# Edge attributes padded to 128 weight rows, and row numbers copied amid the gathers of the group before

## The reference, cut to what matters

```python
def transformer_conv(h, edge_index, edge_attr, Wq, bq, Wk, bk, Wv, bv, We, ...):
    q, k, v = (h @ W.T + b  for each of the three)     # per node, 4 heads of 32
    e = (edge_attr @ We.T)                              # 4 numbers an edge -> 128
    k_j = k[src] + e
    v_j = v[src] + e
    alpha = einsum('ehc,ehc->eh', q[dst], k_j) / sqrt(32)
    ...                                                 # softmax over the edges of a dst
    out = segment_sum(a * v_j, dst)
```

## Time and profile before

| | |
|---|---|
| time, median of 3 runs | 3711.26 us (3694.59 to 3713.19) |
| the profiled execution | 3716.44 us, of which 3714.7 us are its span |
| busy, share of the span | PE 68%, PEld 51%, DVE 61%, ACT 46%, POOL 62% |
| first-layer edge phase | POOL's first gather 332.8 us, PE's last sum 1447.6 us |
| second-layer edge phase | POOL's first copy 2571.3 us, its last 3092.7 us |
| last node phase | POOL's first copy 3133.4 us, its last 3683.8 us |

### The profile page before, as it was taken

How to read it: one execution, slowest core, us unless ns; L and a number is a source line. 1 busy time by engine, 2 the same in 40 slices (tenths; PEclk the granted TensorE clock), 3 DMA queues, 4 the chain that set the end, 5 groups by cost and what they waited for, 6 DMA issues and landing times. The chain is left out here.

```text
span 3714.7 us, 56727 instructions
## 1 busy us (share of the span) xinstructions
PE 2534.6 (68%) x13730; PEld 1902.9 (51%) x13730; DVE 2276.3 (61%) x9172; ACT 1717.7 (46%) x4075; POOL 2310.2 (62%) x2429
## 2 busy tenths in 40 slices
PE   0004999999999996599999999996333442444444
PEld 0003777777777774366666666664333332444444
DVE  8885555666566656487787878783111111777777
ACT  8993222222222222488787888884111111333332
POOL 5554777777777770555555555543777775777775
PEclk9999999999999997799999999997555555565555
DMA  6452233333333331333333334332666664456666
GB/s 204 172 178 78 79 87 88 93 88 87 86 94 87 88 86 43 74 108 103 107 103 105 106 98 107 103 97 79 121 119 123 123 119 98 127 137 143 137 134 120
DMA packets 253887, 401.92 MB, mean 108 GB/s; under 512 B 56515, under 2 KB 165456, under 8 KB 253728
## 3 DMA queue, kind: packets, MB, share of 16 engines
q1 hardware_dynamic: 183670, 265.77, 25.0%
q0 software_dynamic: 63424, 133.57, 17.9%
q10 hardware_dynamic: 6682, 1.46, 0.2%
HBM read 241.74 MB, written 160.29 MB: 108 GB/s over the span
## 5 line engine op out<-in xcount | busy, mean ns | idle before, releaser
L1629 POOL DMA_INDIRECT aggc<-rows,at_nc x392 | 400.9, 1023 | 149.0 <-issue 109.0
L625 POOL DMA_INDIRECT zs<-z_table,at_s x392 | 381.0, 972 | 161.3 <-issue 89.6
L1147 POOL DMA_INDIRECT agg<-rows,at_n x392 | 389.1, 993 | 144.3 <-issue 111.1
L1463 POOL DMA_INDIRECT h2s<-h_table,at_s x392 | 374.5, 955 | 147.7 <-issue 92.6
L625 POOL DMA_INDIRECT zd<-z_table,at_d x392 | 378.2, 965 | 124.8 <-issue 122.3
L1508 PE MATMUL p_sum<-h2s,same 128*128 128x129 f32 x784 | 213.8, 444 | 338.4 <-DMA h2s<-h_table,at_s 283.3
L1212 PE MATMUL p_f<-z_t,w_t 128*128 128x512 f32 x784 | 377.4, 612 | 64.2 <-ACT act L1282 64.0
L1223 PE MATMUL p_f<-w_t,act 128*128 128x128 f32 x3136 | 383.8, 278 | 0.0
L1223 PEld LDWEIGHTS p_f<-w_t,act 128*128 128x128 f32 x3136 | 361.2, 192 | 22.2 <-issue 22.2
L1508 PEld LDWEIGHTS p_sum<-h2s,same 128*128 128x128 f32 x784 | 176.4, 323 | 375.7 <-issue 300.1
L754 ACT ACTIVATE v_sb<-p_v 128x264 f32<-128x264 f32 x196 | 76.7, 392 | 594.1 <-DVE msgs L836 379.7
(11 more groups left out here) (316 smaller groups left out, 6669.3 us busy)
## 6 DMA issues: line engine op xcount, KB each, us to landing
rows<-rows_sb SPq DMA_DIRECT2D x49, 576.0 KB, 3.6
h_table<-h2b SPq DMA_DIRECT2D x49, 516.0 KB, 2.9
rows<-rows_sb SPq DMA_DIRECT2D x49, 516.0 KB
xa<-in_x_dram SPq DMA_DIRECT2D x49, 512.0 KB, 3.8
z_table<-za SPq DMA_DIRECT2D x49, 512.0 KB, 2.9
dst_sb<-dst SPq DMA_DIRECT2D x98, 256.0 KB
xb<-in_x_dram SPq DMA_DIRECT2D x49, 512.0 KB, 4.1
x_table<-x1b SPq DMA_DIRECT2D x49, 512.0 KB, 4.8
```

Of the source, the lines that this page charges most:

```text
L625: pool.indirect_dma_start(out=to[:, slot, k], out_offset=None, in_=z_table, in_offset=bass.IndirectOffsetOnAxis(ap=at[:, slot, k:k + 1], a ...
L1147: pool.indirect_dma_start(out=agg[:, ring, k], out_offset=None, in_=rows0, in_offset=bass.IndirectOffsetOnAxis(ap=at_n[:, ring, k:k + 1], ...
L1463: pool.indirect_dma_start(out=h2s[:, slot, k], out_offset=None, in_=h2_table, in_offset=bass.IndirectOffsetOnAxis(ap=at_s[:, slot, k:k + 1 ...
L1629: pool.indirect_dma_start(out=agg[:, slot, k], out_offset=None, in_=rows1, in_offset=bass.IndirectOffsetOnAxis(ap=at_n[:, slot, k:k + 1], ...
```

## The change

`wea`, `metag` and `ea_tr` get 16 partitions or columns a tile in place of 6 (`EW = P // G = 16`), so that `ea_tr` fills 128 partitions; the ten further columns of each tile in `metag`, and the further rows in `wea`, hold zeros, set once at the phase's start. On POOL, the copy of the row numbers becomes a function of its own (`index`), and is done for the next group amid the gathers of the present one: after 8 of 16 DMAs in the first edge phase, after 6 of 8 in the second, and ahead of the 8 in the last node phase.

```diff
+EW = P // G
-        wea = sb("wea", [G * META, G, D + DV])
+        wea = sb("wea", [P, G, D + DV])
...
-            metag = t("metag", [P, 2, G, META])
+            metag = t("metag", [P, 2, G, EW])
-            ea_tr = t("ea_tr", [G * META, 2, P])
+            ea_tr = t("ea_tr", [P, 2, P])
-            p_alpha, p_back, p_ea = ..., p_small[0:G * META, 256:256 + P]
+            p_alpha, p_back, p_ea = ..., p_small[:, 256:256 + P]
...
-                    def gather(g, slot, use):
+                    def index(g, slot, use):
                         for u in range(4):
                             at_least(pool, gathered[slot][u], 64 * use)
                         nc.gpsimd.tensor_copy(at_s[:, slot], ...).then_inc(at_ready, 1)
                         nc.gpsimd.tensor_copy(at_d[:, slot], ...).then_inc(at_ready, 1)
-                        for u in range(4):
+
+                    def gather(g, slot, use, parts):
+                        for u in parts:
                             at_least(pool, turned, 4 * g + u - 7)
                             pool.wait_ge(at_ready, 2 * g + 2)
...
-                    pipeline(pool, NGE, 1, lambda new: gather(*new))
+                    def half(ahead, new):
+                        if new:
+                            gather(*new, (0, 1))
+                        if ahead:
+                            index(*ahead)
+                        if new:
+                            gather(*new, (2, 3))
+                    pipeline(pool, NGE, 2, half)
...
-                        act.dma_start(wea[j * META:(j + 1) * META, j, :], wea1[:]).then_inc(wea_done, 16)
+                        act.dma_start(wea[j * EW:j * EW + META, j, :], wea1[:]).then_inc(wea_done, 16)
-                            v.tensor_copy(metag[:, slot], meta[:, bass.ds(g * G, G)]).then_inc(meta_ready, 1)
+                            v.tensor_copy(metag[:, slot, :, 0:META], meta[:, bass.ds(g * G, G)]).then_inc(meta_ready, 1)
+                    chain.mark(v.memset(metag[:], 0.0))
... the second edge phase
-                    pipeline(pool, NGE, 1, gather)
+                    def half(ahead, new):
+                        if new:
+                            gather(*new, (0, 1, 2))
+                        if ahead:
+                            index(*ahead)
+                        if new:
+                            gather(*new, (3,))
+                    pipeline(pool, NGE, 2, half)
... the last node phase
-                    pipeline(pool, NGN, 1, gather, WAYS)
+                    def half(ahead, new):
+                        if ahead:
+                            index(*ahead)
+                        if new:
+                            gather(*new)
+                    pipeline(pool, NGN, 2, half, WAYS)
```

More of the change, by code:

```diff
@@ L594, in build @@
             p_v, p_small, p_sum, p_deg = ps("p_v"), ps("p_small"), ps("p_sum"), ps("p_deg")
-            p_alpha, p_back, p_ea = p_small[0:G * H, 0:P], p_small[:, P:P + 2 * G * H], p_small[0:G * META, 256:256 + P]
+            p_alpha, p_back, p_ea = p_small[0:G * H, 0:P], p_small[:, P:P + 2 * G * H], p_small[:, 256:256 + P]
             gathered = [[s(f"gathered{a}{b}") for b in range(4)] for a in range(2)]
@@ L1452, in _, with index @@
                 def _(pool):
-                    def gather(new):
-                        g, slot, use = new
+                    def index(g, slot, use):
                         for u in range(4):
@@ L1619, in _, with index, gather @@
                 def _(pool):
-                    def gather(new):
-                        g, slot, use = new
+                    def index(g, slot, use):
                         at_least(pool, agg_in[slot], 16 * G * use)
                         nc.gpsimd.tensor_copy(at_n[:, slot], node_row[:, bass.ds(g, 1), :].rearrange("p a t -> p (a t)")).then_inc(S["at_ready"], 1)
+                    def gather(g, slot, use):
                         at_least(pool, S["base_ready"], g - WAYS + 1)
```

## The result

| | before | changed |
|---|---|---|
| time, median | 3712.23 us (3694.59 to 3713.99, 4 runs) | 3557.59 us (3554.38 to 3560.11, 4 runs) |
| ratio, 95% interval | | 0.9592 (0.9565 to 0.9618) |
| the profiled execution | 3716.44 us, span 3714.7 | 3554.38 us, span 3552.5 |

The kernel is 4.1% faster. The two profiled spans differ by 162.2 us, where the sum said 138; 7 us of that are chance, since the execution profiled before stood 4.2 us over its median and the one after 3.2 us under its own.

The account below looks back on a forecast made before the run. PE was taken to bound the first edge phase at 22.0 us a group, POOL close behind, and POOL the second edge and last node phases. 84 + 27 + 27 = 138 us off 3716.4 gives 3578, as median 3573; range 3548 to 3630.

Parts of the forecast that it names:

- ten matmuls of a step: First edge phase, PE: with 128 weight rows throughout, a step's matmuls go from 3.70 to 2.25 us, 1.45 saved.
- PE's own need a group: First edge phase: PE's time for a group of four steps falls by 5.8 us, from 22.0 to 16.2.
- POOL a group, first edge phase: Sixteen DMAs at 15.49 us, fifteen gaps at 4.5, one gap with both copies at 0.57: 20.6 us.
- from PE's last turn to its last sum: End of first edge phase: two steps of projections remain and get 2.9 us shorter, so 22.1 becomes 19.2 us.
- gain, first edge phase: PE ends the phase at 1363 us in place of 1447.6, as POOL sets the pace: 84 us.
- gain, second edge phase: POOL's group edge shrinks from 1.01 to 0.46 us, 0.55 saved in each of 49 groups: 27 us.
- gain, last node phase: The same POOL edge as in the second edge phase, 0.55 us saved in each of 49 groups: 27 us.
- The handover from PE to POOL: First edge phase: PE at 16.2 us a group falls well under POOL at 20.6, so POOL sets the pace.
- the unknown gap behind a copy: On POOL, from a row-number copy to the next DMA, which doesn't read it: 0.25 us, between 0.19 and 0.30.
- Another chain: First edge phase: work handed between PE, DVE and ACT holds a group at 21.3 us, giving 3607 us; chance 15%.
- The padding worthless: First edge phase: PE stays at 22.0 us a group, only the later phases' 54 us remain, 3657 us; chance 5%.
- The copies waiting: Second edge phase: gathered rows take over 7.5 us to land, POOL stops, that gain goes, 3600 us; chance 4%.
- Slower by the clock: First edge phase: PE partly at half clock; at a share of 0.6, 25.9 us a group, 3848 us; chance 2%.

Follow-up runs that it names:

- the first sitting: Padding alone, copies alone, 64 and 96 weight rows, run on one chip, where the kernel before the change took 4227.66 us.

## Why the prediction was right, and where it was off

| term of the sum | predicted | measured |
|---|---|---|
| ten matmuls of a step | 3.70 to 2.25 us | 2.24 |
| PE's own need a group | 16.2 us | 15.9, with half the gathers left out |
| POOL a group, first edge phase | 20.6 us | (1332.5 - 331.5) / 48.9 = 20.5 |
| from PE's last turn to its last sum | 22.1 to 19.2 us | 21.6 |
| gain, first edge phase | 84 us | 88.6 |
| gain, second edge phase | 27 us | 37 |
| gain, last node phase | 27 us | 39 |

The three measured gains are 2 us more than the 162.2 of the spans, since what lies between the first two phases took 1.7 us longer.

**The padding.** Right in place and size. The step that mattered was to read the starts of the products and not the durations of the weight loads. The Trainium skill, "TensorE: Matmul & The Clock Gate", section on LDWEIGHTS, has loads of 32 and of 128 rows take the same time. The trace agrees on the durations, 189 and 197 ns, and the rule taken as a price of the products, 3657 us, is refuted by 3558. "TensorEngine Tiling (Array Packing)" of the same skill, Key Properties, says that "Changing tiling mode (not just tile) drains the TensorE". The runs fit it if a product with 48 or 64 weight rows counts as another mode and one with 96 doesn't; that is a reading, and no run looked at the mode.

**The handover from PE to POOL.** Right, and it is the main point of the case. The two halves alone gain 54 and 0 us in the first edge phase, 88.6 together. Over the whole kernel the medians give 47 us for the padding and 68 for the copies, 116 by addition, and 155 with both. The 39 us beyond the sum (35 in the first edge phase alone) are the stretch in which POOL can go below 21.2 us only if PE goes below it too.

**The copies: right mechanism, size too small.** The prediction took 0.25 us for the unknown gap behind a copy, "the middle" of 0.19 and 0.30. It is 0.16, below both its bounds; a copy costs 0.06 us beyond a plain gap, and 0.65 is saved a group, not 0.55. That is 2 x 49 x 0.10 = 10 us of the miss in the second and the last phase. The first phase's edge took 0.49 us where 0.57 was put, 4 us in all. The rest of the second phase's surplus is 5 us. The waits for PE fell there from 16.1 to 9.4:

```profile
POOL h2s L1476 <- PE p_sum L1529: 9.4, 31, 0.3
```

but these 31 are plain gaps, none over 0.3 us, that happen to end behind PE. What is gone are two long gaps between DMAs, with 1.9 us the longest, 3.3 us beyond plain ones; and the DMAs themselves took 1.6 us less.

In the last phase the surplus is 39 - 32 = 7 us, and some of it is luck: from first to last gather the phase took 560.4 to 563.4 us in the three traces with the old edges, and 521.5 to 527.8 in the seven with the new ones, the changed kernel's being the shortest. The DMAs' own durations, 398 to 404 us in all, make most of that spread. The second edge phase is 521.4 / 48 = 10.86 us a group before, by its copies, and (2979.3 - 2485.4) / 391 x 8 = 10.11 after, by the starts of its gathers; the last 11.47 and 10.67 in the same way.

**The end of the first edge phase.** POOL's last gather ended at 1332.5 + 0.95 + 0.30 + 0.95 = 1334.7, not 1342, and the last turn followed 2.7 us later, with 2 predicted. The tail behind it was off by 2.4 us: the two remaining steps were to get 2.9 us shorter, and it went from 22.1 to 21.6. The clock did that. PE now comes to its last turn out of a wait of 2.19 us for rows, and eight of the ten products behind it run at the half level; PE's timeline of the changed kernel:

```profile
1338.12 0.64 PE L689 MATMUL p_qk<-wkv_t,z_t 128*128 128x128 f32 x2
1338.55 0.63 PE L690 MATMUL p_qk<-wea,ea_tr 128*128 128x128 f32 x2
...
1349.46 0.51 PE L705 MATMUL p_deg<-is_hi,is_lo 128*128 128x391 bf16 x2 [2.44 <-DVE is_hi L838]
```

The starts are 0.43 us apart, where they are 0.22 at full clock; the granted clock is 0.60 from 1337 to 1341 us, and was 1.00 from 1424 to 1428 in the kernel before. From the last turn to the end of that step it is 4.37 us, where it was 4.14 and should have been 2.69: 1.7 us. The second step saved its 1.46 in full, PE's waits of 2.44 and 2.01 us for DVE's comparisons are what they were, and the last sums, more of them at the lower clock, took 0.7 us more. What made the clock fall there isn't shown: a wait as long, 2.48 us at 799 us, left it full. Together 1359.0 in place of 1363: POOL ended 7 us earlier than forecast, and the tail gave 2.4 of them back, so the two errors in part cancelled.

**The rivals.** Another chain: refuted by the run without destination gathers. The padding worthless: refuted. The copies waiting: not with six or eight DMAs of cover; the mechanism is real, as the run without cover shows. The landing time is no one number: 1.9 us behind the end of the issue where POOL stood still, but with POOL issuing on, as in the copies alone, where the trace has the landing of 96 gathers of `h2s`, it goes up to 6.8 us behind the start of the issue, 5.8 behind its end (7.0 in the run without destination gathers, with 48 to read):

```profile
DMA to landing us min/median/max: 2.5/2.7/6.8
```

The 3.1 that was read off PE lies in that range, and the cover of 7.5 us was little more than the slowest took. Slower by the clock: the granted clock was 0.99 in the window of the changed kernel, the full level nearly throughout, with PE busy 116 of 150 us; only the phase's end paid for it, as above. With the padding alone it was 0.90 with PE busy 118.72 of 150, so some of that window was at the half level; it cost nothing that shows, as PE waited for gathers anyway.

## What to carry to other kernels

Read the distance between the starts of matmuls, not the durations of their weight loads: what a neighbour of another shape costs shows there, and padding with zeros to the neighbours' shape removes it, a mere reordering half of it. When two engines are within a few per cent of each other, try the two repairs together before dropping either; in the first edge phase each alone gave 54 or 0 us of the 89. A copy that feeds a DMA belongs between DMAs that don't read it, and behind its slot's former readers by more than their landing time: without cover it cost 114 us in a phase, behind two DMAs 14, behind six nothing.

## What the runs showed of the hardware

- On PE, going between 128 weight rows and 48 or 64, either way, costs 0.18 to 0.20 us in float32 at full clock; between 128 and 96 nothing. The durations of the weight loads don't show it (189 ns on the average with 48 rows, 197 with 128); those of the products do in part (a pass with 48 rows 329 ns on the average in the kernel before, 281 with 128 in the changed one), and the starts in full.
- On POOL, a DMA starts 0.16 us behind a copy that it doesn't read, 0.30 behind another DMA, and 0.81 behind a copy for which it must wait. Behind a copy that had itself waited for a gather it was 0.70, though the DMA didn't read it, and 0.16 to 0.68 behind a copy with 2.5 us of cover.
- A gather of 128 rows of 516 bytes lands 1.5 to 7.0 us behind the end of its issue (144 gathers of `h2s` in two runs), 1.9 where POOL waited for it.
- PE's products of 128 columns in float32 start 0.22 us apart at full clock and 0.43 at the half level.
- The kernels of the first sitting took 11 to 17% longer than the same ones later: padding alone 4067.79 for 3666.73 us, copies alone 4279.14 for 3645.59, 96 rows 4120.5 for 3556.86. Of the profiled executions' difference, 295 of 385 us (padding) and 444 of 654 (copies) had arisen when the last gather of `zs` began. In the first edge phase about half of it is idle time of PE with the copies alone (211 of 450 us) and two thirds with the padding alone (206 of 318); the rest is work at a lower granted clock (0.77 for 1.00, and 0.84 for 0.91). The cause is open: each sitting had a chip of its own, so chip and hour can't be told apart.
